# Fetching 13 instead of 11 gather tiles a layer through SyncE's queue, nine rows a slot

## The reference, cut to what matters

```
for l in range(L):                                  # L = 2
    xn = layernorm(x); xp = xn + pos
    q = (xp @ Wq + bq); k = (xp @ Wk + bk); v = (xp @ Wv + bv)    # [3125, 8, 16]
    att = einsum('ehd,ehd->eh', q[dst], k[src]) / 4
    att = nan_to_num(clip(att, -50, 50))
    ex = exp(att - segment_max(att, dst)[dst])
    alpha = ex / (segment_sum(ex, dst)[dst] + 1e-16)
    aggr = segment_sum((v[src] * alpha[:, :, None]).reshape(-1, 128), dst)
    x = x + aggr @ Wo + bo
    x = x + gelu(layernorm(x) @ W1 + b1) @ W2 + b2
```

## Time and profile before

| | |
|---|---|
| runs shown, median (lowest to highest) | 2099.82 us (2099.09 to 2101.54) |
| the profiled execution's own time | 2100.35 us |
| its span | 2098.6 us |
| mean granted TensorE clock | 0.945 |
| PE, DVE, ACT, POOL busy | 1715.5, 1770.0, 1206.7, 1506.9 us |
| gathers by POOL | 1542 |
| rows by SP | 2816 |

### The profile page before, as it was taken

The page is one execution under the profiler, slowest core; times in us unless marked ns, Lnnn a source line. Parts: engine busy times, 40 slices in busy tenths (PEclk is TensorE's granted clock), DMA queues, the critical chain, the costliest instruction groups (busy, mean ns, idle before and its releaser), DMA issues.

```text
span 2098.6 us, 47279 instructions
## 1 busy us (share of the span) xinstructions
PE 1715.5 (82%) x10627; PEld 1468.3 (70%) x10627; DVE 1770.0 (84%) x5031; ACT 1206.7 (58%) x2827; POOL 1506.9 (72%) x1601
## 2 busy tenths in 40 slices
PE   4878889788988898798776877988797888888876
PEld 4667777677777777677656766867676767767775
DVE  8758998989898989889877788888888888887985
ACT  8325566565757575565554545656464656456554
POOL 7177777777777777777727777777777777777773
PEclk9979999999999999999988998999999999999987
DMA  3366666666666666566425655666566666656641
GB/s 91 110 196 180 207 197 189 200 183 189 192 195 183 194 185 188 177 184 191 148 79 168 187 184 170 198 182 187 182 186 183 183 184 183 187 178 187 187 145 55
DMA packets 211522, 365.80 MB, mean 174 GB/s; under 512 B 38972, under 2 KB 147216, under 8 KB 211248
## 3 DMA queue, kind: packets, MB, share of 16 engines
q0 software_dynamic: 74464, 203.13, 34.0%
q10 hardware_dynamic: 85360, 81.57, 12.8%
q1 hardware_dynamic: 51424, 78.08, 11.1%
HBM read 350.93 MB, written 8.40 MB: 171 GB/s over the span
## 4 chain that ended last, share of the span: by engine, by line
POOL 34%; issue 19%; DVE 19%; PE 12%; DMA 8%; ACT 6%; DVEq 1%; SPq 0%; ACTq 0%
POOL kvr L925 34%; DVE agg L1909 6%; DMA kvr<-kv_table,srcidx 4%; DMA x_nat<-kv_table 3%; PE bank L1203 3%; PE bank L1234 3%; PE bank L1216 3%; DVE kvr L1515 2%; DVE onehot L1860 2%; DVE prod L1874 1%; ACT apart L1433 1%; DVE msg L1898 1%; DVEq L672 1%; ACT L1476 1%; PE bank L1160 1%
## 5 line engine op out<-in xcount | busy, mean ns | idle before, releaser
L925 POOL DMA_INDIRECT kvr<-kv_table,srcidx x1542 | 1466.4, 951 | 526.4 <-issue 459.3
L1203 PE MATMUL bank<-q,onehotT 128*128 x3320 | 494.4, 296 | 274.2 <-DVE prod L1874 134.0
L1203 PEld LDWEIGHTS bank<-q,onehotT 128*128 128x128 f32 x3320 | 441.1, 204 | 366.6 <-issue 354.3
L1476 ACT ACTIVATE bank<-attc 128x32 f32<-128x32 f32 x404 | 81.3, 201 | 782.5 <-DVE attc L1889 779.3
L1909 DVE TENSOR_TENSOR agg<-agg,bank 128x136 f32 x1624 | 472.2, 291 | 50.8 <-PE bank L1216 26.6
L1216 PE MATMUL bank<-msg,onehot 128*128 128x136 f32 x3320 | 486.6, 293 | 1.0 <-DVE msg L1898 0.8
L1216 PEld LDWEIGHTS bank<-msg,onehot 128*128 128x128 f32 x3320 | 448.0, 204 | 3.0 <-DVE msg L1898 2.8
L1874 DVE TENSOR_TENSOR prod<-kvr,bank 128x512 f32<-128x512 f32 (+1 forms) x404 | 272.9, 676 | 180.4 <-DMA kvr<-kv_table,srcidx 133.5
L1234 PE MATMUL bank<-loops 128*128 128x256 f32 x1200 | 296.4, 390 | 29.2 <-DMA loops<-kv_table 25.7
L1234 PE MATMUL bank<-x_nat 128*128 128x256 f32 x1200 | 294.1, 387 | 31.6 <-DMA x_nat<-kv_table 27.6
L1433 ACT ACTIVATE apart<-relT,minus_p 128x512 bf16<-128x512 bf16 x416 | 294.0, 707 | 15.2 <-issue 14.8
(11 more groups left out here) (230 smaller groups left out, 1352.9 us busy)
## 6 DMA issues: line engine op xcount, KB each, us to landing
relT<-rel_table SPq DMA_DIRECT2D x104, 512.0 KB
kv_rows<-kv_table SPq DMA_DIRECT2D x2816, 1.0 KB
x_nat<-kv_table ACTq DMA_DIRECT2D x144, 256.0 KB
loops<-kv_table ACTq DMA_DIRECT2D x144, 256.0 KB
kvr<-kv_table,srcidx POOLq DMA_INDIRECT x1542
loop_kv<-kv_table SPq DMA_DIRECT2D x25, 128.0 KB
kv_table<-qkv SPq DMA_DIRECT2D x25, 128.0 KB
kv_table<-onehot SPq DMA_DIRECT2D x8, 256.0 KB, 2.2
```

The source lines that it names most:

```text
L925: pool.indirect_dma_start(kvr[:, n % RING, j, :], None, kv_table[l], bass.IndirectOffsetOnAxis(ap=srcidx[:, step:step + 1], axis=0)).then_ ...
L1203: mm = pe.matmul(bank[2][:, j * D:(j + 1) * D], onehotT[:, m % OHT, j, :], q[:, bass.ds(ranks[j + h], 1), :].rearrange("p a c -> p (a c)") ...
```

## The change

11 groups a layer had a tile of rows: group 23 and 41, 58, ... 194, each 17 apart, eight rows in each of 16 slots. Now there are 13: 18, 33, ... 198, each 15 apart, nine rows in each of 14 slots and two in a fifteenth. A tile's last slot is followed at once by the next tile's first, from slot 0 to slot 194. GpSimd gathers 1538 tiles in place of 1542, SyncE fetches 3328 rows in place of 2816.

The rest of the diff lets the picks be given for each layer apart, with a width for each; the lists and widths given are the ones of before. Three things differ in what is issued: pick_table has a line for each layer's passes and is filled by 24 DMAs of two partitions each (before 12 lines, 24 DMAs of one); pick_apart is a tensor of its own instead of a part of x_nat or loops; and ScalarE waits on s_pick_apart, which only ScalarE itself counts up, before it loads the next pick_src.

```
-ROW_GROUPS = [23] + [41 + 17 * i for i in range(10)]
-ROWS_A_SLOT = 8
+ROW_GROUPS = [18 + 15 * i for i in range(13)]
+ROWS_A_SLOT = 9
 ROW_SLOTS = -(-P // ROWS_A_SLOT)
...
-PICK_GROUPS = [24 + 15 * i for i in range(12)]
+PICK_GROUPS = [[24 + 15 * i for i in range(12)] for _ in range(L)]
 PICKS = 2
-PICK_STEPS = -(-BLOCKS // 2)
-PICK_AHEAD = PICK_STEPS + 3
+PICK_WIDTH = (2, 2)
+PICK_STEPS = [-(-BLOCKS // width) for width in PICK_WIDTH]
...
-        pick_table = nc.dram_tensor("pick_table", [len(PICK_GROUPS), PICKS * P], F32, kind="Internal").ap()
+        pick_table = nc.dram_tensor("pick_table", [pick_pass(L, 0), PICKS * P], F32, kind="Internal").ap()
...
+        pick_apart = sb("pick_apart", [P, PICKS * P], BF16)
...
-            sp.wait_ge(s_pick_table, 16 * PICKS * len(PICK_GROUPS))
+            sp.wait_ge(s_pick_table, 16 * pick_pass(L, 0))
...
-            for i, g in enumerate(PICK_GROUPS):
-                for j in range(PICKS):
-                    c, row = divmod(row_of(g, at_begin=True) + G - PICKS + j, P)
-                    act.dma_start(pick_table[i:i + 1, j * P:(j + 1) * P], step_src_f[row:row + 1, c * P:(c + 1) * P]).then_inc(s_pick_table, 16)
+            for i, g in enumerate(PICK_GROUPS[0] + PICK_GROUPS[1]):
+                c, row = divmod(row_of(g, at_begin=True) + G - PICKS, P)
+                act.dma_start(pick_table[i:i + 1, :].rearrange("a (j e) -> (a j) e", j=PICKS), step_src_f[row:row + PICKS, c * P:(c + 1) * P]).then_inc(s_pick_table, 16)
...
-                if t == PICK_STEPS - 1 and i + 1 < len(PICK_GROUPS):
-                    act.wait_ge(s_pick_hot_dve, (k + 1) * (BLOCKS // 2))
-                    act.dma_start(pick_src[l], pick_table[i + 1:i + 2, :].broadcast_to([P, PICKS * P])).then_inc(s_pick_src, 16)
+                if t == PICK_STEPS[l] - 1 and i + 1 < len(PICK_GROUPS[l]):
+                    act.wait_ge(s_pick_hot_dve, hots_by(l, i, BLOCKS - 1, False))
+                    act.wait_ge(s_pick_apart, hots_by(l, i, BLOCKS - 1, True))
+                    act.dma_start(pick_src[l], pick_table[pick_pass(l, i + 1):pick_pass(l, i + 1) + 1, :].broadcast_to([P, PICKS * P])).then_inc(s_pick_src, 16)
```

More of the change, by code:

```diff
@@ L173, in gathers, with pick_pass, pick_step, pick_blocks @@
     return min(G, TILES - n % GROUPS * G)
-PICK_GROUPS = [24 + 15 * i for i in range(12)]
+PICK_GROUPS = [[24 + 15 * i for i in range(12)] for _ in range(L)]
 PICKS = 2
-PICK_STEPS = -(-BLOCKS // 2)
-PICK_AHEAD = PICK_STEPS + 3
+PICK_WIDTH = (2, 2)
+PICK_STEPS = [-(-BLOCKS // width) for width in PICK_WIDTH]
 def by_pick(n):
-    return n % GROUPS in PICK_GROUPS
+    return n % GROUPS in PICK_GROUPS[n // GROUPS]
 def pick_turn(n):
     l, g = step_of(n)
-    return l * len(PICK_GROUPS) + PICK_GROUPS.index(g)
+    return pick_pass(l, PICK_GROUPS[l].index(g))
 def pick_at(n):
     l, g = step_of(n)
-    for i, to in enumerate(PICK_GROUPS):
-        if 0 <= g - (to - PICK_AHEAD) < PICK_STEPS:
-            return l * len(PICK_GROUPS) + i, g - (to - PICK_AHEAD)
+    for i, to in enumerate(PICK_GROUPS[l]):
+        t = g - (to - PICK_STEPS[l] - 3)
+        if 0 <= t < PICK_STEPS[l]:
+            return (l, i), t
     return None, None
+def pick_pass(l, i):
+    return sum(len(groups) for groups in PICK_GROUPS[:l]) + i
+def pick_step(l, i, t):
+    return sum(len(PICK_GROUPS[k]) * PICK_STEPS[k] for k in range(l)) + i * PICK_STEPS[l] + t
+def pick_blocks(l, t):
+    return range(t * PICK_WIDTH[l], min(BLOCKS, (t + 1) * PICK_WIDTH[l]))
+def hot_by_act(l, b):
+    return b % 2 == 0
+def hots_by(l, i, upto, by_act):
+    whole = sum(len(PICK_GROUPS[k]) * sum(hot_by_act(k, b) == by_act for b in range(BLOCKS)) for k in range(l))
+    return whole + i * sum(hot_by_act(l, b) == by_act for b in range(BLOCKS)) + sum(hot_by_act(l, b) == by_act for b in range(upto + 1))
 def by_rows(n):
@@ L445, in build @@
         pick_src = [t[:, 0:PICKS * P] for t in spare]
-        pick_kv = [t[:, 2 * P:2 * P + 4 * KV].rearrange("p (u h c) -> p u h c", u=2, h=2) for t in spare]
-        pick_hot = [t[:, 2 * P + 4 * KV:2 * P + 8 * KV].rearrange("p (u h c) -> p u h c", u=2, h=2) for t in spare]
-        pick_apart = [t[:, 2 * P + 8 * KV:3 * P + 8 * KV].bitcast(BF16) for t in spare]
+        pick_kv, pick_hot = ([t[:, 2 * P + k * 2 * width * KV:2 * P + (k + 1) * 2 * width * KV].rearrange("p (u h c) -> p u h c", u=2, h=width) for t, width in zip(spare, PICK_WIDTH)] for k in range(2))
         spare = q[:].rearrange("p b c -> p (b c)")
@@ L646, in build, with pick_src_loaded @@
         iota_ps = bank[0][:, P:2 * P]
-        def pick_src_loaded(k):
-            l, i = divmod(k, len(PICK_GROUPS))
-            return (s_pick_src, 16 * (l * (len(PICK_GROUPS) - 1) + i)) if i else (s_pick_first, 16 * (l + 1))
+        def pick_src_loaded(l, i):
+            return (s_pick_src, 16 * (pick_pass(l, i) - l)) if i else (s_pick_first, 16 * (l + 1))
         picked = bank[7][:, 0:PICKS * KV]
@@ L750, in first_pick_src @@
                     sp.wait_ge(s_looped, NCH)
-                sp.dma_start(pick_src[l], pick_table[0:1, :].broadcast_to([P, PICKS * P])).then_inc(s_pick_first, 16)
+                sp.dma_start(pick_src[l], pick_table[pick_pass(l, 0):pick_pass(l, 0) + 1, :].broadcast_to([P, PICKS * P])).then_inc(s_pick_first, 16)
             first_pick_src(0)
@@ L834, in _ @@
                     first_pick_src(1)
-                    sp.wait_ge(s_pick_kept, len(PICK_GROUPS))
+                    sp.wait_ge(s_pick_kept, len(PICK_GROUPS[0]))
                     load_x0()
@@ L1219, in pick @@
             def pick(k, t):
[L1221 to L1224, removed]
+                l, i = k
+                m = pick_step(l, i, t)
+                if t == 0 and pick_pass(l, i):
+                    pe.wait_ge(s_pick_kept, pick_pass(l, i))
+                if t == 0 and i == 0:
                     pe.wait_ge(s_agg, sums_by(l * GROUPS + SEAM_GROUPS))
                 pe.wait_ge(s_pick_kv[m % 2], 16 * (m // 2 + 1))
[L1227 to L1230, removed]
+                for h, b in enumerate(pick_blocks(l, t)):
+                    if hot_by_act(l, b):
+                        pe.wait_ge(s_pick_hot_act, hots_by(l, i, b, True))
                     else:
-                        pe.wait_ge(s_pick_hot_dve, k * (BLOCKS // 2) + t + 1)
+                        pe.wait_ge(s_pick_hot_dve, hots_by(l, i, b, False))
                     for j in range(PICKS):
@@ L1439, in pick_hots @@
             def pick_hots(k, t):
-                l, i = divmod(k, len(PICK_GROUPS))
-                m, b = k * PICK_STEPS + t, 2 * t
-                nb = min(2, BLOCKS - b)
+                l, i = k
+                m, blocks = pick_step(l, i, t), pick_blocks(l, t)
                 if t == 0:
-                    act.wait_ge(*pick_src_loaded(k))
+                    act.wait_ge(*pick_src_loaded(l, i))
                 if m >= 2:
@@ L1454, in pick_hots @@
                             act.wait_ge(s_table[buffer(l, c)], stored(l, c))
[L1455 to L1460, removed]
-                if t == PICK_STEPS - 1 and i + 1 < len(PICK_GROUPS):
-                    act.wait_ge(s_pick_hot_dve, (k + 1) * (BLOCKS // 2))
-                    act.dma_start(pick_src[l], pick_table[i + 1:i + 2, :].broadcast_to([P, PICKS * P])).then_inc(s_pick_src, 16)
+                act.dma_start(pick_kv[l][:, m % 2, 0:len(blocks), :], kv_table[l].rearrange("(b p) c -> p b c", p=P)[:, blocks.start:blocks.stop, :]).then_inc(s_pick_kv[m % 2], 16)
+                for h, b in enumerate(blocks):
+                    if hot_by_act(l, b):
+                        made = hots_by(l, i, b, True) - 1
+                        if made:
+                            act.wait_ge(s_pick_hot_act, made)
+                        act.activation(pick_apart[:], pick_src[l], ACT.Abs, bias=minus_node[:, b:b + 1]).then_inc(s_pick_apart, 1)
+                        act.wait_ge(s_pick_apart, made + 1)
+                        act.activation(pick_hot[l][:, m % 2, h, :], pick_apart[:], ACT.Relu, bias=1.0, scale=-1.0).then_inc(s_pick_hot_act, 1)
+                if t == PICK_STEPS[l] - 1 and i + 1 < len(PICK_GROUPS[l]):
+                    act.wait_ge(s_pick_hot_dve, hots_by(l, i, BLOCKS - 1, False))
+                    act.wait_ge(s_pick_apart, hots_by(l, i, BLOCKS - 1, True))
+                    act.dma_start(pick_src[l], pick_table[pick_pass(l, i + 1):pick_pass(l, i + 1) + 1, :].broadcast_to([P, PICKS * P])).then_inc(s_pick_src, 16)
             def pick_keep(n):
                 k = pick_turn(n)
-                act.wait_ge(s_picked, PICK_STEPS * (k + 1))
+                act.wait_ge(s_picked, pick_step(step_of(n)[0], PICK_GROUPS[step_of(n)[0]].index(step_of(n)[1]) + 1, 0))
                 act.wait_ge(s_msg, n - RING + 1)
@@ L1479, in edge_exp @@
                 act.activation(msg[:, n % 2, 0:t, D:AGG], attc[:, n % 2, 0:t * H].rearrange("p (j h) -> p j h", h=H), ACT.Exp).then_inc(s_den, 1)
-            act.wait_ge(s_pick_table, 16 * PICKS * len(PICK_GROUPS))
```

(12 more changed lines are left out.)

## The result

The changed kernel takes **2429.28 us** (median of three, 2428.66 to 2432.48) against 2099.82: a ratio of 1.1574, 95% interval 1.1558 to 1.159. I had forecast 2135, in a range of 2097 to 2165. The direction was right and the size wrong by a factor of more than nine (329 us slower, where I had said 35).

A forecast was written before the change was run, and what follows sets the result against it. GpSimd's gathers were taken to bound the kernel before, SyncE's rows layer 0 after the change. Profiled 2100.35 us, + 36 for layer 0, - 1.2 for layer 1, gave 2135 us; range 2097 to 2165.

The forecast's parts named there:

- GpSimd's gathers bound the kernel before: Layer 0: 771 gathers one behind the other, 1.25 us each, set its end; SyncE waits only 93.7 us in 923.
- The ninth register: SyncE's load of nine node numbers a slot: 0.20 us more than eight; lower end 0.055, upper end plus 1.4.
- Rival C: Register loads of nine go one by one, perhaps where misaligned: 2570 us, about 2250 if half the slots; chance 0.10.
- my sum: SyncE's layer 0: start 144.2, 13 tiles x 69.3 = 900.9, other jobs 55.3; last row out at 1100.4 us.
- Slot times, the start of layer 0 and the jobs among the rows: SyncE, layer 0: slot of nine 4.83 us, start 144.2, refills 17.2, loop_kv 20.1, table stores 18.0 us.
- 5 us to spare: Layer 1: SyncE's last row lands at 2056.1, group 198 is due at 2061.3, so GpSimd bounds; 1.25 us gained.
- VectorE could make it up ... what counts is its end: Layer 0: late row tiles first stall VectorE alone, which could recover; SyncE's end counts, layer 0 ending 36 us later.
- rival B: Ninth number nearly free (0.055 us): slot 4.69, tile 67.2, layer 0's last row 11.5 us late; 2110 us; chance 0.15.
- Rival D: SyncE keeps up, four gathers fewer save 1.25 to 2.5 us a layer: 2095.4 to 2098 us; chance 0.15.
- The landing of the last row: End of layer 0: SyncE's last row lands some 2.0 us after it goes out, at 1102.4 us.

The follow-up runs named there:

- the kernel with nine of twelve: Changed kernel, still nine rows a slot, but each load takes twelve numbers from a multiple of four and uses nine: 2135.67 us, ratio 1.0174.
- eights and twelves: Changed kernel with 13 slots of eight rows and two of twelve a tile, every load starting at a multiple of four: 2109.54 us, ratio 1.0047.
- SyncE out of the way: Changed kernel's 13 tiles a layer, with 16 rows in every second slot or 32 in every fourth: 2098.77 us (ratio 0.9997) and 2098.16 us (0.9993).

## Why the prediction was wrong, point by point

- **GpSimd's gathers bound the kernel before, SyncE had under 15% to spare in layer 0**: right in the main. GpSimd was not the bound in the first part of layer 0 (the point on VectorE below), and the 93.7 us leave out 22.2 of waits at L715, after the last row; 115.9 of 923 are still under 15%. Right too was that SyncE would become the bound, by how it would show (VectorE at the rows, GpSimd at a full ring), and that the rest of the diff is nothing.
- **The ninth register** is the step that failed. I took 0.20 us more for each of the 14 loads, "two fours and one". That holds at the four that begin at a multiple of four: 1.01 against 0.78 us, 0.23 more. The ten others go one by one, 2.13 us: 1.35 more than eight aligned, where my upper end said 1.4. Rival C had this mechanism and even this condition ("not where a slot's first address is no multiple of four"), at a chance of 0.10 and outside the range. Every row of four numbers or more that I weighed began at a multiple of four, so they couldn't tell the two cases apart; I took their agreement for evidence about the other kind.
- With the measured loads **my sum gives the end of layer 0's rows**: a tile is 69.3 + 10 x 1.12 = 80.5 us, 13 of them 1046.5; layer 0's last row leaves at 144.2 + 1046.5 + 55.3 = 1246.0 (measured 1247.7). Rival C's own number for a part of the slots, "half of them, about 2250", was a wrong sum: with 7 of 14 at its 6.03 us a tile is 77.7, SyncE ends layer 0 148 us late and layer 1 251, and the time is 2351.
- **Slot times, the start of layer 0 and the jobs among the rows**: right, by the kernel with nine of twelve: 954.3 us for the rows of layer 0 with all that lies among them against 956.2, begun 2.0 us earlier than I had said, and 2135.67 us against the recorded 2135. That the total agrees to 1 us is in part luck; against its own runs of the kernel before it is 37.4 us slower, where I had said 34.8.
- **Layer 1, "5 us to spare"**: wrong in the changed kernel (327.9 - 185.3 = 142.6 us more lost there), right at aligned loads: no late tile.
- **"VectorE could make it up ... what counts is its end"**: wrong. With eights and twelves SyncE ended layer 0 on time and the kernel still lost 11 us by the medians. My rival B had 2110 for such slots, by a late end that wasn't there. The error goes back to the first paragraph: I took GpSimd for the bound of all of layer 0 because it never waited, and didn't look at whether VectorE ever waited for GpSimd, which it did not until 762.9 us.
- **Rival D's gain** of up to 5.0 us for four gathers: not seen. With SyncE out of the way the medians moved by 1.5 us at most, and the intervals, 0.9988 and 0.9983 at their low ends, leave room for 2.5 and 3.6 us. That VectorE and not GpSimd bounds much of layer 0 would explain one half of it; I have not shown that.
- **The landing of the last row**: I took 2.0 us; from its issue's end to the product that waits for it pass 1.1 us. Harmless here.

## What to carry to other kernels

A bound on an unseen cost is only as wide as the conditions of the rows behind it: before pricing a new size, look at what else the size changes. Here nine in place of eight moved the address of ten loads in fourteen, and that was worth 294 us, where all the rest of the change together, two tiles more a layer and the ninth number, was worth some 36. And an engine that never waits need not be the bound: ask also whether the engine behind it ever waits for it, and how much. Those waits, here 19.7 us near the end of layer 0, are about all the room that the second engine has for a stall, however early the stall comes.

## What the runs showed of the hardware

- A register load on SyncE from SBUF takes about 0.08 + 0.056 us a number if it begins at a multiple of four 4-byte numbers and their count is one too (0.52 for 8, 0.75 for 12, 0.97 for 16, 1.87 for 32, shortest each). One number left over adds 0.2 us (nine: 1.01 against 0.78, medians). If the load begins elsewhere, it takes 0.2 us for each number beyond the first (1.67 for 8, 1.87 for 9, shortest each). The medians, mostly behind another issue, are 0.2 to 0.26 longer. Beginning two numbers past a multiple of four is no better than one or three (2.13 each for nine).
- The Trainium skill (Runtime: NRT & Kernel Launch, Instruction fetch mechanics) gives about 200 ns a register even in bulk; it describes loads from HBM, and the numbers here lie in SBUF. The runs agree for loads that begin off a multiple of four (202 ns a number, from 1.67 for 8 to 1.87 for 9), and not for the others (56 ns).
- A 1 KB row lands soon after its issue: in most of the 26 tiles of the changed kernel 1.1 us pass from the end of the last issue to the product that had waited for it, 2.3 at the most.
